# Softmax shifts of two causal attentions: made by GpSimd instead of VectorE, the second half's maximum seeded with the first's

## The chip, the cores and the metric

The kernel runs on one core of one Trainium2 chip. The metric is the device time of one execution in microseconds (us); lower is better. Engines are called as in the profile: PE is TensorE (PEld its weight loads), DVE is VectorE, ACT is ScalarE, POOL is GpSimd, SP is SyncE, which issues the DMAs.

## What is computed

A chain of six blocks over x of shape (2, 1024, 512), in fp32. Two of them are causal self-attentions, and only these are touched:

```python
x = x + 0.5 * ffn(layernorm(x))          # low-rank corrected product, scaled per column
x = x + attention_0(layernorm(x))        # 32 query heads of 16, 8 key heads, rotary: "rot"
x = x + 0.5 * ffn(layernorm(x))
x = x + 0.5 * moe(layernorm(x))          # 8 experts of rank 16, top 2
x = x + attention_1(layernorm(x))        # 8 heads of 32: "std"
x = x + 0.5 * moe(layernorm(x))
# inside an attention, per head:
scores = q @ k.T * scale; scores = where(causal, scores, -big)
out = softmax(scores) @ v
```

## The kernel before

The two batches run one after the other, with the six blocks in sequence. All five engines run programs of their own, in an order written out by hand, and meet through semaphores. An attention treats its heads in units: rot has 8 units of 4 heads, std 4 units of 2 heads. For each unit there are two streams of work.

**The stream of scores.** Twelve steps per unit: 4 for the first half of the queries (c=0), 8 for the second (c=1), each step one block of 128 keys. In a step TensorE makes transposed scores (`score`, L742 in rot, L736 in std), ScalarE takes their exponential (L1149), GpSimd sets to zero what is above the diagonal, in steps on the diagonal only (`affine_select`, L1301), and two steps later (rot) or three (std) TensorE multiplies by the values (`value`, L758). In this layout a query is a column, so the row maximum can't be subtracted by an operand of the exponential. It enters as two further rows of the queries' operand, a high and a low part ("the shifts"), which are multiplied by ones on the keys' side.

**The stream of maxima.** For those shifts the maximum of each query row has to be known before its scores are made, about one unit ahead. TensorE makes the scores once more in the other layout (`ring_item`, L660) into three PSUM banks that are used in turn ("the ring"), and VectorE reduces each bank to a column of `maxes`: by `tensor_reduce` (L949) where no mask is needed, or by a fused add of the causal mask and maximum (L945, a main instruction and a read of the accumulator) where the bank holds the diagonal. A query tile t has one bank set for the first 512 keys (kp=0) and, for t of 4 to 7, a second one for the rest (kp=1, always masked). In a rot unit that is 16 `tensor_reduce` of 512 columns and 32 masked ones, 16 of them with kp=1; in a std unit 8, 16 and 8.

After the last bank of t=3 (c=0) and of t=7 (c=1) of a unit, `shift_parts` makes the shifts of those four query tiles from `maxes`, on VectorE: for c=1 first the maximum of the two halves (L981, 128x16 in rot), then the negative rounded to the short format (L985), then what the rounding left (L987). An item of the ring ("shift") has TensorE transpose them (L665), VectorE copy them out (L958) and SP write them as rows into the queries' operand (L490). The item stands `SHIFT_DELAY` banks behind the bank that it depends on. Items "norm" divide finished heads by their sums (L670 on TensorE, L965 and L970 on VectorE).

`plan_ring` writes the order of the ring's items against the steps: `ring_first` before the first step (12 banks and `SHIFT_DELAY` and a slack of 12 in rot, 6 and the same in std), then three slots per step. TensorE takes the items in that order between its `score` and `value`, and waits for VectorE to have read the item three before it (`ring_free`).

## Time and profile before

| what | value |
|---|---|
| median of 3 runs | 1426.17 us (1425.89 to 1436.26) |
| the profiled execution | 1425.2 us, of which the span of its instructions is 1423.5 us |
| PE busy | 1298.5 us, 91% |
| DVE busy | 963.8 us, 68% |
| ACT busy | 630.8 us, 44% |
| POOL busy | 485.5 us, 34% |
| rot attention | about 137 to 402 us and 837 to 1100 us |
| std attention | about 555 to 650 us and 1250 to 1348 us |
| granted TensorE clock, mean | 0.933 of full speed |

The busy time is an average over very different stages. The rot attentions, more than a third of the time, have two engines busy over 90% of the time side by side; the layers between them have TensorE alone. A granted clock of 1.00 is 2.4 GHz and of 0.50 is 1.2 GHz.

### The profile page before, as it was taken

What the parts mean: (1) busy time and instruction counts of PE and PEld (TensorE: products, weight loads), DVE (VectorE), ACT (ScalarE), POOL (GpSimd) and SP (SyncE); (2) the same over time, 40 slices, a digit from 0 to 9 for tenths busy, and PEclk for the clock granted to TensorE, in tenths of its full rate; (3) what the DMA queues carried; (4) which work ended last, traced back from release to release, by engine and by line L of the source; (5) the groups of instructions that cost most, each with busy time, mean ns of one, the idle gap of its engine ahead of it and who ended that gap; (6) DMA issues with size and microseconds to landing.
All of it is one profiled execution on the core that took longest, in us unless ns stands there. A gap on an engine that the chain in (4) does not pass through costs nothing.

```text
span 1423.5 us, 21475 instructions
## 1 busy us (share of the span) xinstructions
PE 1298.5 (91%) x7328; PEld 799.1 (56%) x7328; DVE 963.8 (68%) x2846; ACT 630.8 (44%) x929; POOL 485.5 (34%) x734
## 2 busy tenths in 40 slices
PE   4997999999899898998879889999988999999898
PEld 1875544444277686445658754444434877854366
DVE  5765898899257845644758467999871787376276
ACT  1245366666622245443212544766665222634421
POOL 1574032221255442116426621311223653311261
PEclk8999599999999998999989975999999999989999
DMA  9200000110011000000130000010100100000001
GB/s 299 88 1 30 2 2 2 32 32 3 1 35 37 1 1 30 2 1 5 55 144 1 24 8 2 3 32 2 32 3 1 56 15 1 31 2 2 1 16 45
DMA packets 19932, 38.50 MB, mean 27 GB/s; under 512 B 4416, under 2 KB 6208, under 8 KB 19712
## 3 DMA queue, kind: packets, MB, share of 16 engines
q1 hardware_dynamic: 19824, 37.12, 7.8%
q8 instruction: 60, 0.98, 0.3%
q14 instruction: 48, 0.39, 0.1%
HBM read 31.21 MB, written 11.01 MB: 30 GB/s over the span
## 4 chain that ended last, share of the span: by engine, by line
PE 68%; DVE 17%; POOL 5%; issue 5%; ACT 3%; DMA 2%; SPq 0%; DVEq 0%; ACTq 0%; POOLq 0%
PE bank L758 15%; PE bank L660 12%; PE bank L587 7%; PE bank L589 7%; PE bank L588 7%; DVE maxes L949 5%; PE bank L742 4%; PE bank L640 4%; PE bank L736 3%; DVE unused L945 3%; PE bank L567 2%; PE bank L622 2%; PE bank L670 2%; POOL probs L1221 2%; DVE x L847 1%
## 5 line engine op out<-in xcount | busy, mean ns | idle before, releaser
L1149 ACT ACTIVATE probs<-bank 128x1024 f32<-128x1024 f32 (+3 forms) x416 | 368.0, 911 | 301.5 <-PE bank L742 192.5
L660 PE MATMUL bank<-ops 48*128 48x512 f32 (+3 forms) x960 | 323.5, 441 | 13.3 <-DVE maxes L949 4.1
L945 DVE CUSTOM_DVE_ANT_0 unused<-bank,causal 128x128 bf16<-128x128 f32 (+3 forms) x640 | 279.4, 486 | 73.0 <-PE bank L660 69.8
L1301 POOL TENSOR_SCALAR_AFFINE_SELECT probs<-probs 128x256 f32<-128x256 f32 (+1 forms) x256 | 118.8, 464 | 587.6 <-ACT probs L1149 587.3
L660 PEld LDWEIGHTS bank<-ops 48*128 48x128 f32 (+1 forms) x960 | 164.2, 208 | 198.1 <-DVE maxes L945 79.6
L758 PE MATMUL bank<-probs,v_mem 128*17 128x512 f32 (+6 forms) x1920 | 256.1, 524 | 6.1 <-ACT heads_raw L1138 5.6
L949 DVE TENSOR_REDUCE maxes<-bank 128x1 f32<-128x512 f32 x320 | 207.3, 684 | 40.3 <-PE bank L660 38.8
L1051 ACT CAST xT<-bank 128x512 fp32r<-128x512 f32 (+1 forms) x128 | 71.2, 560 | 271.7 <-PE bank L567 271.7
L742 PE MATMUL bank<-ops 50*128 50x512 f32 (+2 forms) x640 | 178.5, 454 | 4.9 <-ACT probs L1149 4.8
L822 DVE TENSOR_TENSOR xT<-bank,xT 128x512 fp32r<-128x512 f32 (+1 forms) x128 | 83.5, 655 | 125.0 <-ACT xT L1051 124.9
L587 PE MATMUL bank<-w_odd_hi,xT 128*128 128x512 f32 (+1 forms) x384 | 155.4, 405 | 1.9 <-DVE xT L822 1.9
L589 PE MATMUL bank<-w_odd_hi,xT 128*128 128x512 f32 (+1 forms) x384 | 138.0, 359 | 0.0
L588 PE MATMUL bank<-w_odd_lo,xT 128*128 128x512 f32 (+1 forms) x384 | 137.7, 359 | 0.0
L742 PEld LDWEIGHTS bank<-ops 50*128 50x128 f32 x640 | 88.0, 200 | 58.2 <-ACT probs L1149 29.7
L1106 ACT CAST ops<-bank 128x512 fp32r<-128x512 f32 x144 | 81.7, 587 | 65.9 <-PE bank L640 65.7
L587 PE MATMUL bank<-ops,xT 128*128 128x512 f32 x224 | 100.3, 448 | 4.0 <-DVE x L847 1.6
L640 PE MATMUL bank<-identf,features 128*128 128x128 f32 x512 | 78.5, 290 | 19.5 <-POOL heads_raw L1258 13.9
L1191 POOL TENSOR_SCALAR var_eps<-mv 128x1 f32<-128x1 f32 x96 | 38.9, 405 | 159.1 <-DVE mv L805 158.9
L589 PE MATMUL bank<-ops,xT 128*128 128x512 f32 x224 | 90.1, 402 | 0.0
L588 PE MATMUL bank<-ops,xT 128*128 128x512 f32 x224 | 89.8, 401 | 0.0
L758 PEld LDWEIGHTS bank<-probs,v_mem 128*17 128x17 f32 (+1 forms) x1920 | 41.0, 99 | 78.0 <-issue 52.6
L640 PEld LDWEIGHTS bank<-identf,features 128*128 128x128 f32 x512 | 62.4, 147 | 37.7 <-POOL heads_raw L1258 17.3
(109 smaller groups left out, 1896.1 us busy)
## 6 DMA issues: line engine op xcount, KB each, us to landing
w_odd_lo<-staging_wqkv SPq DMA_DIRECT2D x4, 1536.0 KB, 6.7
x<-x_dram SPq DMA_DIRECT2D x16, 256.0 KB, 5.9
out_dram<-x SPq DMA_DIRECT2D x16, 256.0 KB, 2.0
staging_wqkv<-wqkv_dram SPq DMA_DIRECT2D x2, 1536.0 KB, 14.0
ops<-staging_dora SPq DMA_DIRECT2D x3, 1024.0 KB, 5.5
ops<-shiftT SPq DMA_DIRECT2D x160, 4.0 KB
w_odd_lo<-staging_wo SPq DMA_DIRECT2D x2, 1024.0 KB, 5.2
ops<-staging_base SPq DMA_DIRECT2D x2, 1024.0 KB, 5.5
```

What stands on the lines that cost most here:

```text
L587: mm(dst, x_hi[:, k, :], hi[:, k, :], start=(k == 0), stop=False)
L588: mm(dst, x_hi[:, k, :], lo[:, k, :], start=False, stop=False)
L589: last = mm(dst, x_lo[:, k, :], hi[:, k, :], start=False, stop=(k == kc - 1 and not lora))
L640: last = nc.tensor.transpose(dst[:, k * P:(k + 1) * P], src, identf[:])
L660: last = mm(dst[:, h * w:(h + 1) * w], queries(a, u)[rows, t // 4, hi, t % 4 * P:(t % 4 + 1) * P], keys(a, u, hi)[rows, HALF * kp:HALF * k ...
L742: last = mm(dst, keys(a, u, 0)[rows, block], queries(a, u)[rows, c, heads_of[0]:heads_of[-1] + 1, columns], start=True, stop=True)
L758: last = mm(heads[a.head_rows * h:a.head_rows * h + a.dim + 1, q0 - HALF * c:HALF], v[:, j, a.kv_head(u, r, i), :], probs[:, e % 6, n, fir ...
L822: V.tensor_tensor(xT[:, n % 2, 1, 0:kc, :], turn[n % 2][:, 0:kc * P].rearrange("p (k c) -> p k c", k=kc), xT[:, n % 2, 0, 0:kc, :].bitcast ...
L945: V.tensor_tensor_reduce(unused[:, masked % 3, 0:w], part, causal[:, HALF - w:], 1.0, NEG, ALU.add, ALU.max, dst).then_inc(s["max_done"].s ...
L949: V.tensor_reduce(dst, part, AX.X, ALU.max).then_inc(s["max_done"].sem, 1)
L1149: A.activation(probs[:, e % 6, :, 0:cols], scores[:, 2 * (e % 2):2 * (e % 2) + 2, 0:cols], ACT.Exp, scale=a.scale).then_inc(s["exp"].sem, 1)
L1301: G.affine_select(out=p, in_=p, compare_op=ALU.is_ge, fill=0.0, base=0, pattern=pattern, channel_multiplier=-1).then_inc(s["masked"].sem, 1)
```

## The change

`shift_parts` moves from VectorE's program to GpSimd's. Its work there is three instructions for each half: minus the maximum into a new buffer `minus_max`, a cast of it to the short format (the high part), and the difference of the two (the low part). GpSimd makes them in its `attention` loop, after the masks of the step in which the half's last bank was put into the ring (`maxima_by_step`); those of banks in `ring_first` it makes before its first mask. It waits for that bank's maxima (`max_done`), and from the second unit on also for the transposition of the unit before (`ring_full`).

The combining maximum (L981) is gone. Instead the masked maximum of kp=1 starts from the one that kp=0 gave for the same head and tile: the immediate start value `NEG` becomes a column of `maxes`, which VectorE reads per partition, behind a further wait on its own `max_done`.

`SHIFT_DELAY` goes from 3 to 5, so a shift item stands two banks later in the ring, and `ring_first` is two banks longer.

```diff
-SHIFT_DELAY = 3
+SHIFT_DELAY = 5
...
                 if n + 1 in self.max_banks_of:
+                    self.maxima_by_step[step[0]].append((u, self.max_banks_of.index(n + 1)))
                     due_m.append([(u, self.max_banks_of.index(n + 1)), SHIFT_DELAY])
...
-                                V.tensor_tensor_reduce(unused[:, masked % 3, 0:w], part, causal[:, HALF - w:], 1.0, NEG,
+                                above = NEG
+                                if kp == 1:
+
+                                    m0 = a.max_bank_of(t, 0, head)
+                                    dve.wait_ge(s["max_done"].sem, s["max_done"].at(b, u * a.unit_max_ops + a.max_ops_to[m0]))
+                                    above = maxes[:, u % 2, 0, a.heads.index(head), t:t + 1]
+                                V.tensor_tensor_reduce(unused[:, masked % 3, 0:w], part, causal[:, HALF - w:], 1.0, above,
                                                        ALU.add, ALU.max, dst).then_inc(s["max_done"].sem, 1)
...
-                        if n + 1 in a.max_banks_of:
-                            shift_parts(b, st, u, a.max_banks_of.index(n + 1))
...
-                if c == 1:
-                    V.tensor_tensor(mx, mx, maxes[:, u % 2, 1, 0:nh, 4:8], ALU.max).then_inc(s["shift_step"].sem, 1)
-                    dve.wait_ge(s["shift_step"].sem, s["shift_step"].at(b, 3 * u + 2))
...
-                V.tensor_scalar(hi, mx, -1.0, None, ALU.mult).then_inc(s["shift_step"].sem, 1)
-                dve.wait_ge(s["shift_step"].sem, s["shift_step"].at(b, 3 * u + 1 + 2 * c))
-                V.scalar_tensor_tensor(lo, mx, -1.0, hi.bitcast(F32), ALU.mult, ALU.subtract).then_inc(s["shift"].sem, 1)
...
+            def shift_parts(b, st, u, c):
+
+                a, s = ATT[st], qs[st]
+                nh, m = a.unit_heads, a.unit_heads * 4
+                ch = 2 * u + c
+                mx = maxes[:, u % 2, c, 0:nh, 4 * c:4 * c + 4]
+                pool.wait_ge(s["max_done"].sem, s["max_done"].at(b, u * a.unit_max_ops + a.max_ops_to[a.max_banks_of[c] - 1]))
+                if ch >= 2:
+
+                    pool.wait_ge(s["ring_full"].sem, s["ring_full"].at(b, a.ring.index(("shift", u - 1, c)) + 1))
...
+                G.tensor_scalar(minus, mx, -1.0, None, ALU.mult).then_inc(s["shift_step"].sem, 1)
+                pool.wait_ge(s["shift_step"].sem, s["shift_step"].at(b, 2 * ch + 1))
+                G.tensor_copy(hi, minus).then_inc(s["shift_step"].sem, 1)
+                pool.wait_ge(s["shift_step"].sem, s["shift_step"].at(b, 2 * ch + 2))
+                G.tensor_tensor(lo, minus, hi.bitcast(F32), ALU.subtract).then_inc(s["shift"].sem, 1)
...
+                    for unit, c in a.maxima_by_step[g + 1]:
+                        shift_parts(b, st, unit, c)
```

How this moves instructions, at three places. In these rows `unused,maxes<-bank,causal` is the masked maximum (its second row reads the accumulator), and L958, L960, L964 and so on are lines of the changed file where it is of the change.

VectorE, the end of a rot unit's maxima (t=7, kp=1) and the start of the next, before:

```order
L945 ISA unused,maxes<-bank,causal 128x512 [waits rot_max_done,rot_ring_full]
L945 ISA maxes 128x1
L945 ISA unused,maxes<-bank,causal 128x512 [waits rot_max_done,rot_ring_full]
L945 ISA maxes 128x1
L981 TENSOR_TENSOR maxes<-maxes 128x4x4 [waits rot_max_done]
L985 TENSOR_SCALAR shifts<-maxes 128x16 [waits rot_shift_step]
L987 SCALAR_TENSOR_TENSOR shifts<-maxes,shifts 128x16 [waits rot_shift_step]
L945 ISA unused,maxes<-bank,causal 128x128 [waits rot_max_done,rot_ring_full]
```

and of the change:

```order
L960 ISA unused,maxes<-bank,causal,maxes 128x512 [waits rot_max_done,rot_ring_full]
L960 ISA maxes 128x1
L960 ISA unused,maxes<-bank,causal,maxes 128x512 [waits rot_max_done,rot_ring_full]
L960 ISA maxes 128x1
L960 ISA unused,maxes<-bank,causal,maxes 128x512 [waits rot_max_done,rot_ring_full]
L960 ISA maxes 128x1
L960 ISA unused,maxes<-bank,causal 128x128 [waits rot_max_done,rot_ring_full]
L960 ISA maxes 128x1
```

The three small instructions are gone, and the masked maxima of kp=1 have `maxes` among what they read.

TensorE, step 4 of a rot unit (the shift of the next unit's c=0), before, where L660 is a bank of the ring, L665 the transposition of the shifts, L742 a score, L758 a value:

```order
L742 MATMUL bank<-ops 128x512 [waits rot_exp_done,rot_shift_rows1]
L742 MATMUL bank<-ops 128x512
L660 MATMUL bank<-ops 128x512 [waits rot_max_done] x2
L665 MATMUL bank<-identf,shifts 32x128 [waits rot_shift_ready,rot_heads_ready]
L742 MATMUL bank<-ops 128x512 [waits rot_exp_done]
L742 MATMUL bank<-ops 128x512
L660 MATMUL bank<-ops 128x512 [waits rot_max_done]
L758 MATMUL bank<-probs,v_mem 17x256 [waits rot_exp_done,rot_masked]
```

and of the change, with L669, L674, L751 and L767 in their places:

```order
L751 MATMUL bank<-ops 128x512 [waits rot_exp_done,rot_shift_rows1]
L751 MATMUL bank<-ops 128x512
L669 MATMUL bank<-ops 128x512 [waits rot_max_done] x2
L751 MATMUL bank<-ops 128x512 [waits rot_exp_done]
L751 MATMUL bank<-ops 128x512
L669 MATMUL bank<-ops 128x512 [waits rot_heads_ready]
L767 MATMUL bank<-probs,v_mem 17x256 [waits rot_exp_done,rot_masked]
L767 MATMUL bank<-probs,v_mem 17x256 x3
L669 MATMUL bank<-ops 128x128 [waits rot_max_done]
L669 MATMUL bank<-ops 128x128
L674 MATMUL bank<-identf,shifts 32x128 [waits rot_shift_ready,rot_max_done]
```

The transposition stands two banks later, behind a score, a value and their waits.

GpSimd, the first masks of the first rot attention, before:

```order
L1301 AFFINE_SELECT probs<-probs 128x2x128 [waits rot_exp_done] x4
L1301 AFFINE_SELECT probs<-probs 128x4x128 [waits rot_exp_done]
L1301 AFFINE_SELECT probs<-probs 128x2x256 [waits rot_exp_done]
L1301 AFFINE_SELECT probs<-probs 128x2x128 [waits rot_exp_done] x4
L1301 AFFINE_SELECT probs<-probs 128x4x128 [waits rot_exp_done]
```

and of the change:

```order
L1294 TENSOR_SCALAR minus_max<-maxes 128x16 [waits rot_max_done]
L1296 CAST shifts<-minus_max 128x16 [waits rot_shift_step]
L1298 TENSOR_TENSOR shifts<-minus_max,shifts 128x16 [waits rot_shift_step]
L1318 AFFINE_SELECT probs<-probs 128x2x128 [waits rot_exp_done] x4
L1294 TENSOR_SCALAR minus_max<-maxes 128x16 [waits rot_max_done]
L1296 CAST shifts<-minus_max 128x16 [waits rot_shift_step]
L1298 TENSOR_TENSOR shifts<-minus_max,shifts 128x16 [waits rot_shift_step]
L1318 AFFINE_SELECT probs<-probs 128x4x128 [waits rot_exp_done]
L1294 TENSOR_SCALAR minus_max<-maxes 128x16 [waits rot_ring_full,rot_max_done]
L1296 CAST shifts<-minus_max 128x16 [waits rot_shift_step]
L1298 TENSOR_TENSOR shifts<-minus_max,shifts 128x16 [waits rot_shift_step]
L1318 AFFINE_SELECT probs<-probs 128x2x256 [waits rot_exp_done]
```

Three instructions stand ahead of the first mask; further threes stand behind the masks of steps 1, 2 and 10, and from the second unit on behind those of steps 2 and 10.

## Rows read from the trace of the kernel before

**Rows 1.** The page: span, busy time and share of each engine.

```profile
span 1423.5 us, 21475 instructions
...
PE 1298.5 (91%) x7328; PEld 799.1 (56%) x7328; DVE 963.8 (68%) x2846; ACT 630.8 (44%) x929; POOL 485.5 (34%) x734
```

**Rows 2.** Windows, four units: us; busy PE, PEld, DVE, ACT, POOL; clock; DMA.

```profile
307.65:335.89 28.24, 27.48 (x197) 11.70 (x197) 26.28 (x91) 19.00 (x22) 5.79 (x13) 1.00 0.13 41
...
1003.35:1032.76 29.41, 28.86 (x197) 12.07 (x197) 26.29 (x92) 18.99 (x22) 5.80 (x13) 0.94 0.13 38
...
248.78:279.39 30.61, 30.05 (x197) 12.41 (x197) 26.48 (x92) 18.97 (x22) 5.80 (x13) 0.89 0.12 37
...
607.03:628.93 21.90, 20.71 (x104) 10.31 (x102) 14.88 (x52) 10.66 (x14) 3.26 (x9) 1.00 0.00 1
```

**Rows 3.** Windows, stretches inside a rot unit and at rot's start (columns likewise).

```profile
318.01:327.97 9.96, 9.49 (x66) 4.56 (x69) 9.76 (x30) 7.57 (x9) 0.00 (x0) 1.00 0.04 14
...
329.31:339.99 10.68, 10.49 (x81) 4.17 (x77) 9.98 (x38) 7.12 (x8) 3.53 (x8) 1.00 0.01 2
...
137.30:161.90 24.60, 22.68 (x62) 12.91 (x65) 24.28 (x86) 6.13 (x7) 2.27 (x5) 0.54 0.01 2
```

**Rows 4.** Chain that ended last, 335 to 350 us: start, us, what.

```profile
336.24 0.81 PE bank L758 x8
...
339.03 0.56 PE bank L758 x8
```

**Rows 5.** Timeline, all engines, 335.6 to 338.4 us: start, us, engine, line.

```profile
335.88 0.64 POOL L1301 TENSOR_SCALAR_AFFINE_SELECT probs<-probs 128x512 f32<-128x512 f32 x1 [1.84 <-ACT probs L1149]
...
335.89 0.65 DVE L981 TENSOR_TENSOR maxes<-maxes 128x16 f32<-128x16 f32 x1
...
336.98 0.64 POOL L1301 TENSOR_SCALAR_AFFINE_SELECT probs<-probs 128x512 f32<-128x512 f32 x1 [0.46 <-ACT probs L1149]
...
337.64 0.28 PE L665 MATMUL bank<-identf,shifts 128*32 128x128 f32 x1
```

**Rows 6.** Timeline of VectorE, 317.5 to 350 us.

```profile
318.01 1.29 DVE L949 TENSOR_REDUCE maxes<-bank 128x1 f32<-128x512 f32 x2 [0.67 <-PE bank L660]
...
339.99 0.56 DVE L945 CUSTOM_DVE_ANT_0 unused<-bank,causal 128x384 bf16<-128x384 f32 x1
...
343.99 0.17 DVE L985 TENSOR_SCALAR shifts<-maxes 128x16 fp32r<-128x16 f32 x1
...
346.26 1.29 DVE L949 TENSOR_REDUCE maxes<-bank 128x1 f32<-128x512 f32 x2 [0.66 <-PE bank L660]
```

**Rows 7.** Chain at the end of rot's last maxima, 360 to 367 us.

```profile
364.16 0.66 DVE maxes L981
...
365.05 0.19 DVE shifts L987
...
365.37 0.27 PE bank L665
```

**Rows 8.** Timeline of GpSimd's mask there.

```profile
364.14 0.64 POOL L1301 TENSOR_SCALAR_AFFINE_SELECT probs<-probs 128x512 f32<-128x512 f32 x1 [1.85 <-ACT probs L1149]
```

**Rows 9.** Single lines on VectorE: duration ns min/median/max, first and last start, forms.

```profile
L985 DVE TENSOR_SCALAR shifts<-maxes x48: 171/175/672, 138.6 to 1324.7; 128x16 fp32r<-128x16 f32 x32, 128x8 fp32r<-128x8 f32 x16
...
L981 DVE TENSOR_TENSOR maxes<-maxes x24: 166/651/656, 155.7 to 1324.5; 128x16 f32<-128x16 f32 x16, 128x8 f32<-128x8 f32 x8
...
L869 DVE TENSOR_SCALAR route<-route x32: 153/154/155, 451.0 to 1416.7; 128x1 f32<-128x1 f32 x32
...
L872 DVE TENSOR_SCALAR gate<-expert_no,top_atf,route x32: 290/291/293, 451.6 to 1417.2; 128x8 f32<-128x8 f32 x32
```

**Rows 10.** Single lines on GpSimd, likewise.

```profile
L1191 POOL TENSOR_SCALAR var_eps<-mv x96: 211/437/808, 20.9 to 1395.0; 128x1 f32<-128x1 f32 x96
...
L1258 POOL TENSOR_TENSOR heads_raw<-probs,heads_raw x16: 442/454/1035, 86.1 to 829.0; 128x128 fp32r<-128x128 f32 x16
```

**Rows 11.** Waits of TensorE: total us, times, longest.

```profile
PE bank L665 <- DVE shifts L987: 7.7, 4, 2.4
```

24 lines of the change are left out of this document (13 added, 11 removed).

## The prediction

> **What bounds the kernel now.** The page comes first: a span of 1423.5 us with PE busy for 91% and DVE for 68% [rows 1]. The second number is a mean over unlike stages, so the next view is the windows of single units. A steady unit of rot takes 28.24 us at full clock, with DVE busy for 26.28 of them and PE for 27.48; a unit of std takes 21.90 us with DVE busy for 14.88 only [rows 2]. So an edit on DVE can count in rot, which has 14 such units of maxima (units 1 to 7 in both batches; unit 0 is made at rot's start), and hardly in std.
>
> Inside a rot unit I read VectorE's timeline for its idle gaps, since a busy engine with gaps is waiting. There are two kinds of stretch. From 318.01 to 327.97 us DVE is busy for 9.76 of 9.96 us; it is in front of this stretch that it waited 0.67 us for PE, so the stretch begins when PE lets it begin and ends when DVE is through: it is DVE's. It holds the maxima of t=4 and t=5 and the start of t=6 [rows 3, 6]. From 329.31 to 339.99 DVE is busy for 9.98 of 10.68 us and waits for PE in between and at the end, while PE is busy for 10.49: this one is PE's [rows 3, 6].
>
> The shift instructions of the old kernel lie in the second kind. L981, L985 and L987 run from 335.89 to about 336.97, and there the chain of work that ended last goes through PE's value matmuls (336.24 for 0.81 us) [rows 4, 5]. The half c=0 runs at 343.99, and behind it DVE stands idle for 0.66 us, until 346.26 [rows 6]. On the chain they are only at a rot attention's start and at the end of its last maxima [rows 7].
>
> **What is removed from VectorE.** Per rot unit five instructions. Each of the plain ones is 0.175 us; L981 is 0.166 us at best and 0.651 in the median [rows 9], where it runs beside a mask of GpSimd that starts within 0.01 us of it [rows 5]. From one to the next go some 0.035 us (from 364.16 to 365.24 the three take 1.08 [rows 7]). That makes 0.45 us for c=0 and 1.05 for c=1, so 1.5 us per unit, 21 us of DVE's time over the 14 units.
>
> The Trainium skill, "SBUF — State Buffer", section "Who interferes with whom", states that a VectorE instruction with two inputs in SBUF and a GpSimd instruction that reads SBUF lock each other out; the 651 against 166 ns agree. By it 0.49 us per unit, 6.8 of the 21, are such a lock, and GpSimd's mask gets its share back too; with DVE's own times alone the sum would have 14 us here.
>
> What is it worth? In a steady unit the work hiding it is PE's, in stretches where PE is busy without a break. DVE will idle 1.2 us instead of 0.1 at 339.99 and 1.1 instead of 0.66 at 346.26. The most that can come back is what PE's weight loads gain by finding their bank free earlier; I take 0.1 us per unit, 1.4 us in all, and 0.7 per unit (10 us) as the bound. At a rot attention's start, 137.3 to 161.9, DVE is busy for 24.28 of 24.60 us [rows 3], and there five instructions at 0.21 us each are saved in full: 1.0 us, twice.
>
> **What is added to VectorE.** The masked maxima of kp=1 now read their start value per partition. No masked maximum of the trace does so. The nearest rows are two `tensor_scalar` lines: with immediates 154 ns on one element (L869) and 175 ns on up to 16 (L985), with two columns as scalars 291 ns on eight elements (L872) [rows 9]. Two such operands cost 116 ns over L985, one 58 if they add up. Lower bound 0, if the fetch lies in the overlap with the accumulator read of the instruction before; upper bound 137 ns, if one operand costs what the pair costs over L869. I take 58, half of the nearest pair.
>
> The Trainium skill, "ScalarE: Activation LUTs", section "What ACT_TABLE_LOAD costs", gives about 93 ns for each such operand on ScalarE; no run here shows that. By it, as an estimate, the next sum would be 10.4 us instead of 6.5.
>
> Sixteen instructions per rot unit get the operand. The eight of t=4 and t=5 lie in DVE's stretch and are paid in full: 8 x 0.058 x 14 = 6.5 us. The eight of t=6 and t=7 lie in PE's stretch, where DVE has gaps, and are free as long as they stay under what the removal gave; at 116 ns they are 0.93 us per unit against 1.05. At a rot attention's start all sixteen are on the path: 0.93 us, twice, which cancels the 1.0 saved there. Std has eight per unit, beside an engine that is idle a third of the time: nothing. The added wait on `max_done` names an instruction at least three before in rot, two in std, each of 0.2 to 0.6 us: long done, nothing.
>
> **What is added to GpSimd.** Three instructions per half, 144 in all. GpSimd is busy for 5.79 of 28.24 us in a rot unit [rows 2], so only the place counts. A `tensor_scalar` on one column is 0.21 us at least and 0.44 in the median, a `tensor_tensor` on 128 columns 0.45 in the median [rows 10]. Three with their waits are between 0.9 and 1.4 us; I take 1.2. Two things stand behind them. The transposition (L665) ran at 337.64 [rows 5]. GpSimd's mask of that step ends at 336.52, the shifts are ready at 337.7, and the order has the transposition two banks later, past 338.3: in time, by over 0.6 us. The next mask, which ran at 336.98, is pushed to 337.7 to 338.4; the value that reads it ran at 339.03 [rows 4, 5]: in time by 0.6. SP's queue, which writes the rows, is asked later by two banks, half a unit or so before the scores need them: nothing.
>
> At the end of an attention's last maxima nothing covers the chain. The shift item follows its bank at once, as nothing is left to put between, and PE waits for it already: four waits, 7.7 us [rows 11]. In rot DVE had it ready at 365.24 [rows 7]; GpSimd starts its mask at 364.14, is through at 364.78 [rows 8] and with the shifts at 366.0: 0.8 us later. In std L981 is not slowed, but most of the mask is over by then; I take 0.7. Together 2 x 0.8 + 2 x 0.7 = 3.0 us.
>
> **Two banks more before the first step.** They move 1.2 us of DVE's work ahead of the first score. In rot DVE is the bound there anyway and does them a step later otherwise. In std it may cost that once per batch; I leave it at nothing.
>
> **The sum.** +6.5 for the operand, 0.0 at rot's starts, +3.0 at the ends, -1.4 for weight loads: +8.1 us. On the profiled execution's 1425.2 that is 1433.3. The median of the runs lies 1.0 above that execution, so the forecast is 1434.
>
> **The granted clock.** In [rows 2] one unit takes 30.61 us at 0.89 and another 29.41 at 0.94, against 28.24 at 1.00, with the same 26.3 to 26.5 us of DVE's work. Of twelve periods between steady units three were of the first kind and two of the second, about 9.5 us in all. The fall to 1.2 GHz comes behind DVE's stretch, in which PE waits much. A stretch half a microsecond longer may bring more of it, a shorter one less. I forecast as many as before, and carry 7 us either way.
>
> **Rivals.**
>
> *The operand is hidden* (chance 0.25, no change). Then the 6.5 goes: +1.6, 1428. For it speaks that the masked maxima overlap with each other's accumulator read; against it that L872 shows a cost at all.
>
> *The removal pays and the clock stays up* (0.12, faster). The operand is hidden, PE takes up to 0.7 us per unit (-10), the 9.5 us of lost clock come back, and the ends cost 3.0: 1426.2 - 16.5, about 1410. Against it: DVE idles where the removal lies [rows 6].
>
> *The operand costs double and spreads* (0.22, slower). At 116 ns the eight in DVE's stretch are 13 us; at 137, with those of t=6 and t=7 half exposed, 15.3 + 7.7 = 23. With the ends, and the clock's 7 in the worse half, 1441 to 1459. It becomes slower by 1% from about 100 ns on. The mechanism is VectorE as the bound of rot's units through t=4 and t=5.
>
> *GpSimd is late* (0.08, slower). If the three take over 1.8 us, the mask behind them misses its value at 339.03, and PE stands in each unit. At the maxima of [rows 10] (0.81, 0.81 and 1.04) they are 2.7 us: 0.9 x 14 + 1.5 x 4 = 19 us on top of the sum, 1453.
>
> The forecast itself has 0.33. That the change doesn't do what it says is out: the order of instructions shows both parts.
>
> **How the numbers follow.** 1% is 14 us, about what a measurement of this kernel can tell from no change. Faster by more: 0.12. Within 1%, 1412 to 1440: the forecast and the hidden operand, 0.58. Slower: 0.22 + 0.08 = 0.30. The range leaves out most of the fast rival and the far end of the slow ones: 1418 to 1450.
>
> **What would show it.** In the changed profile: the masked maxima of kp=1 by some 60 ns longer than those of kp=0 at 128, 256, 384 and 512 columns; DVE's stretch over t=4 and t=5 longer by half a microsecond; rot units at 28.7 us at full clock; DVE's idle time in the second half of a unit up by a microsecond; the waits of L665's successor for GpSimd four times, near 2.8 us each at most in rot, and none elsewhere. It is wrong if kp=1 costs nothing extra, if a steady unit at full clock is under 28 us, or if values wait for masks in every unit.

## The result and the profile after

Six runs of the changed kernel have a median of 1450.47 us (1440.37 to 1466.83), six of the kernel before beside them 1433.15 us (1425.89 to 1436.26). The ratio is 1.0119, with a 95% interval from 1.0079 to 1.0158: slower by 1.2%. Runs more than 1.5% above the fastest of their kernel are left out of every ratio, and of the means further below: one of the six here, two of six in e3, three of twelve in e1 and e5, six of twelve in e9, and at most one elsewhere.

The forecast was 1434 us with a range of 1418 to 1450. The sum said 8 us more than before, and the two medians differ by 17: the sign is right, the size half of what it should be, and the result lies just beyond the 1% within which most of the chance was put. In the absolute time, 7 of the 16 us between 1434 and 1450 come from the base: the forecast stood on three runs with a median of 1426.17, and the six beside the changed kernel have 1433.15.

The profiled execution took 1441.55 us. Its page, span and busy time, to be read beside [rows 1]:

```profile
span 1439.8 us, 21619 instructions
...
PE 1302.8 (90%) x7328; PEld 801.5 (56%) x7328; DVE 953.2 (66%) x2726; ACT 628.6 (44%) x929; POOL 515.2 (36%) x878
```

VectorE has 10.6 us less to do than before and GpSimd 29.7 more, and the kernel is slower. Windows of single units show a part of it. The columns are those of [rows 2]: a rot unit at full clock, the rot unit before it, and a std unit:

```profile
287.50:315.93 28.43, 27.18 (x195) 11.75 (x196) 25.91 (x86) 18.77 (x23) 7.01 (x19) 1.00 0.01 3
256.21:287.50 31.29, 30.26 (x195) 12.90 (x196) 26.29 (x86) 18.88 (x23) 7.02 (x19) 0.84 0.10 34
596.50:619.21 22.71, 21.61 (x108) 10.41 (x107) 14.38 (x46) 10.64 (x15) 4.46 (x14) 1.00 0.01 1
```

Two readings follow. At full clock a rot unit takes 28.43 us against 28.24, so little is lost there. But of the ten periods from unit 2 to unit 7 of the two batches six take 31.3 us at a mean granted clock of 0.84. And a std unit takes 22.71 us against 21.90, at full clock both times, with less on VectorE.

The five periods from unit 2 to unit 7 in one window, first of the changed kernel (first and second batch):

```profile
193.47:344.32 150.85, 145.20 (x971) 62.71 (x972) 130.46 (x430) 94.48 (x112) 37.14 (x94) 0.90 0.05 16
896.63:1047.46 150.83, 145.17 (x971) 62.75 (x972) 130.46 (x431) 94.48 (x112) 37.16 (x94) 0.90 0.05 16
```

and of the kernel before:

```profile
197.37:344.29 146.92, 143.24 (x960) 60.55 (x957) 131.91 (x456) 94.82 (x110) 29.00 (x61) 0.93 0.06 17
...
897.66:1041.16 143.50, 139.98 (x970) 59.05 (x969) 131.46 (x457) 94.64 (x111) 30.24 (x62) 0.98 0.06 17
```

Ten full-clock units are 284.3 us in the changed kernel and 282.4 before; what was measured is 301.7 and 290.4. So 1.9 of the 11.3 us lost here lie at full clock and 9.4 in the clock.

The period from unit 1 to unit 2, just ahead of these, went the other way. First the changed kernel, then the one before, first and second batch each:

```profile
165.41:193.47 28.06, 26.83 (x191) 11.31 (x184) 25.31 (x86) 20.24 (x26) 10.03 (x20) 0.98 0.01 2
868.59:896.63 28.04, 26.81 (x191) 11.29 (x184) 25.30 (x86) 20.23 (x26) 10.03 (x20) 0.99 0.01 2
...
165.41:197.37 31.96, 31.35 (x200) 13.74 (x197) 27.52 (x91) 21.04 (x26) 9.97 (x15) 0.82 0.01 2
864.86:897.66 32.80, 32.49 (x190) 14.58 (x186) 26.49 (x91) 21.04 (x26) 8.76 (x14) 0.72 0.01 2
```

Here the changed kernel is 8.7 us shorter, so over all twelve periods it is behind by 2.6 us of the 16.3 by which the two profiled spans differ. One execution of each kernel therefore doesn't show where the time goes; the experiments below, which have many runs, have to.

The groups of VectorE by shape, where those with `maxes` among the inputs are kp=1:

```profile
L960 DVE CUSTOM_DVE_ANT_0 unused<-bank,causal,maxes 128x512 bf16<-128x512 f32 x80 | 57.0, 746 | 6.2 <-PE bank L669 5.3
...
L960 DVE CUSTOM_DVE_ANT_0 unused<-bank,causal 128x512 bf16<-128x512 f32 x80 | 51.4, 686 | 19.6 <-PE bank L669 19.6
...
L960 DVE CUSTOM_DVE_ANT_0 unused<-bank,causal,maxes 128x128 bf16<-128x128 f32 x80 | 24.4, 341 | 0.3
...
L960 DVE CUSTOM_DVE_ANT_0 unused<-bank,causal 128x128 bf16<-128x128 f32 x80 | 18.8, 287 | 19.8 <-PE bank L669 19.8
```

The operand costs 60 ns at 512 columns and 54 at 128. GpSimd's three instructions stand in the timeline behind the mask that ends at 336.66:

```profile
336.63 0.25 POOL L1294 TENSOR_SCALAR minus_max<-maxes 128x16 f32<-128x16 f32 x1
...
336.95 0.20 POOL L1296 CAST shifts<-minus_max 128x16 fp32r<-128x16 f32 x1
...
337.23 0.22 POOL L1298 TENSOR_TENSOR shifts<-minus_max,shifts 128x16 fp32r<-128x16 f32 x1
337.41 0.65 POOL L1318 TENSOR_SCALAR_AFFINE_SELECT probs<-probs 128x512 f32<-128x512 f32 x1
```

They take 0.82 us from first start to last end, and the next mask runs at 337.41, 1.39 us behind the start of the mask before it; in the kernel before that distance was 1.10 us (335.88 to 336.98, [rows 5]). The waits of TensorE for shifts, beside [rows 11], and for the rows in the std attention (the second is of its weight loads):

```profile
PE bank L674 <- POOL shifts L1298: 11.4, 6, 2.7
...
PE bank L767 <- POOL probs L1318: 0.4, 2, 0.2
```

```profile
PEld bank L745 <- DMA ops<-shiftT: 10.2, 6, 1.9
```

In the kernel before the second wait stood once, for 1.7 us. The timeline of a std unit shows how it comes about:

```profile
591.88 0.28 PE L674 MATMUL bank<-identf,shifts 128*16 128x128 f32 x1
...
592.70 0.27 DVE L971 COPY shiftT<-bank 16x128 f32<-16x128 f32 x1
...
593.00 1.31 SPq L499 DMA_DIRECT2D ops<-shiftT  x2
...
595.48 0.74 PE L745 MATMUL bank<-ops 98*128 98x512 f32 x2 [0.69 <-DMA ops<-shiftT]
...
596.26 1.02 ACT L1147 ACTIVATE probs<-bank 128x1024 f32<-128x1024 f32 x1 [2.38 <-PE bank L745]
```

From the transposition to the first score that reads the rows go 3.6 us. Two banks later in the ring is a step later in std, and the score waits; ScalarE, which waits for that score, stands idle for 2.38 us.

### The profile page after: what moved, and what is told of

Same layout as the page of the kernel before. It is cut to its first block, busy times and chain, and to the rows that moved or that the text cites. A ratio compares the mean times of both kernels' runs of the same rounds, so it can differ in the third digit from the quotient of the medians.

```text
span 1439.8 us, 21619 instructions
## 1 busy us (share of the span) xinstructions
PE 1302.8 (90%) x7328; PEld 801.5 (56%) x7328; DVE 953.2 (66%) x2726; ACT 628.6 (44%) x929; POOL 515.2 (36%) x878
## 4 chain that ended last, share of the span: by engine, by line
PE 68%; DVE 15%; POOL 5%; issue 5%; ACT 4%; DMA 2%; SPq 0%; DVEq 0%; ACTq 0%; POOLq 0%
PE bank L767 14%; PE bank L669 13%; PE bank L596 7%; PE bank L598 7%; PE bank L597 7%; PE bank L751 5%; DVE maxes L964 4%; PE bank L649 4%; PE bank L745 3%; PE bank L576 2%; PE bank L679 2%; PE bank L631 2%; ACT probs L1147 2%; DVE unused L960 2%; DVE x L856 2%
## 5 line engine op out<-in xcount | busy, mean ns | idle before, releaser
L669 PE MATMUL bank<-ops 48*128 48x512 f32 (+3 forms) x960 | 326.5, 441 | 15.1 <-DVE maxes L964 8.4
L669 PEld LDWEIGHTS bank<-ops 48*128 48x128 f32 (+1 forms) x960 | 169.5, 211 | 197.3 <-DVE maxes L960 81.3
L767 PE MATMUL bank<-probs,v_mem 128*17 128x512 f32 (+6 forms) x1920 | 263.4, 536 | 6.2 <-ACT heads_raw L1136 5.2
L964 DVE TENSOR_REDUCE maxes<-bank 128x1 f32<-128x512 f32 x320 | 204.9, 681 | 49.8 <-PE bank L669 49.0
L751 PE MATMUL bank<-ops 50*128 50x512 f32 (+2 forms) x640 | 183.2, 458 | 5.0 <-ACT probs L1147 4.8
L960 DVE CUSTOM_DVE_ANT_0 unused<-bank,causal 128x128 bf16<-128x128 f32 (+3 forms) x320 | 138.2, 487 | 60.8 <-PE bank L669 60.7
L960 DVE CUSTOM_DVE_ANT_0 unused<-bank,causal,maxes 128x128 bf16<-128x128 f32 (+3 forms) x320 | 161.7, 543 | 24.8 <-PE bank L669 23.6
L751 PEld LDWEIGHTS bank<-ops 50*128 50x128 f32 x640 | 89.8, 203 | 57.4 <-ACT probs L1147 30.0
L767 PEld LDWEIGHTS bank<-probs,v_mem 128*17 128x17 f32 (+1 forms) x1920 | 41.7, 100 | 81.2 <-issue 49.9
```

The source lines that it names most:

```text
L669: last = mm(dst[:, h * w:(h + 1) * w], queries(a, u)[rows, t // 4, hi, t % 4 * P:(t % 4 + 1) * P], keys(a, u, hi)[rows, HALF * kp:HALF * k ...
L751: last = mm(dst, keys(a, u, 0)[rows, block], queries(a, u)[rows, c, heads_of[0]:heads_of[-1] + 1, columns], start=True, stop=True)
L767: last = mm(heads[a.head_rows * h:a.head_rows * h + a.dim + 1, q0 - HALF * c:HALF], v[:, j, a.kv_head(u, r, i), :], probs[:, e % 6, n, fir ...
L960: V.tensor_tensor_reduce(unused[:, masked % 3, 0:w], part, causal[:, HALF - w:], 1.0, above, ALU.add, ALU.max, dst).then_inc(s["max_done"] ...
L964: V.tensor_reduce(dst, part, AX.X, ALU.max).then_inc(s["max_done"].sem, 1)
```

## The experiments

Every kernel was timed in five rounds beside the kernel before. "Rot unit" is the distance between two first `tensor_reduce` of neighbouring units, with the mean granted clock of that distance.

**First set: the change taken apart.** e1 has only the delay: `SHIFT_DELAY = 5` in the kernel before.

> The kernel before with SHIFT_DELAY 5 and nothing else: shifts stay on VectorE, no seed. Theory A (the late item): in std the item of the shifts moves from step 12 to step 13 of a unit, its rows land after the scores of step 16 are due, and TensorE waits for the DMA three times per std attention, 0.4 to 0.7 us idle each with ScalarE idle for 2.4; in rot the transposition stands where the ring is full and TensorE idles 0.46 us per unit. Then this kernel alone is 6 to 12 us slower than before. Theory B (the per-partition start value is what costs, as in the prediction): within 2 us of before. Theory C (GpSimd is late): within 2 us of before too, since GpSimd does nothing new.

Measured: ratio 1.0021 [0.9994, 1.0048]. Windows of a rot and of a std unit:

```profile
285.23:313.27 28.04, 26.94 (x195) 11.95 (x196) 26.27 (x92) 18.78 (x23) 5.83 (x12) 1.00 0.01 3
592.66:615.33 22.67, 21.57 (x108) 10.41 (x107) 14.85 (x51) 10.66 (x15) 3.27 (x8) 1.00 0.01 2
```

The delay does two things that nearly cancel: a rot unit gets 0.2 us shorter, a std unit 0.8 longer. The late rows are the delay's, not GpSimd's. The first theory had the waits right, but its total of 6 to 12 us did not come, since it had no gain in rot.

e2 has only the start value: kp=1 seeded, L981 gone, the two other instructions still on VectorE, delay 3.

```diff
-                if c == 1:
-                    V.tensor_tensor(mx, mx, maxes[:, u % 2, 1, 0:nh, 4:8], ALU.max)...
+                                if kp == 1:
+                                    above = maxes[:, u % 2, 0, a.heads.index(head), t:t + 1]
```

> The kernel before with the seeded maximum alone: kp=1 starts from the maximum of kp=0, L981 is gone, the other two shift instructions stay on VectorE, SHIFT_DELAY 3. Theory A: no transfer becomes late in std, and the time is within 4 us of before. Theory B: 60 ns for each of 16 instructions per rot unit against 0.69 us for L981 gone; the eight in VectorE's stretch cost 0.5 us per unit, 14 units, so 4 to 10 us slower, with more of the low clock in units 3 to 5 of rot.

Measured: 1.0171 [1.0146, 1.0195], the largest cost of any part. A rot unit, five of them (unit 2 to 7) and a std unit:

```profile
293.32:322.99 29.67, 29.09 (x195) 12.04 (x195) 27.05 (x92) 19.18 (x23) 5.83 (x12) 0.94 0.05 9
...
200.82:354.57 153.75, 151.00 (x970) 62.91 (x969) 136.09 (x452) 95.56 (x111) 30.39 (x62) 0.88 0.05 16
...
606.13:627.99 21.86, 21.45 (x108) 10.46 (x107) 15.04 (x51) 10.66 (x15) 3.27 (x8) 1.00 0.01 2
```

VectorE has 27.05 us of work against 26.28 in [rows 2], and no steady rot unit of the profiled execution is wholly at full clock. Std is untouched. The ratio stands for 24 us, where the expectation had 4 to 10.

e3 is the changed kernel with `SHIFT_DELAY = 3`, e4 the changed kernel with 5 in rot and 3 in std.

> The changed kernel with SHIFT_DELAY back at 3 in both attentions. Theory A: std is as before the change, the waits for the rows and the 0.46 us per rot unit are gone, so 6 to 12 us faster than the changed kernel (0 to 8 us over before). But the shifts of GpSimd are ready 0.8 us after the mask, so TensorE may wait for them at rot's item, up to 0.5 us per unit, which would eat up to 7 of it. Theory B: as slow as the changed kernel, 14 to 20 us over before.

> The changed kernel with SHIFT_DELAY 3 in std and 5 in rot. Theory A: only the std part is mended, and the waits of std's scores for the rows are gone: 6 to 9 us faster than the changed kernel, so 8 to 11 over before. Theory B: no difference from the changed kernel.

Measured: e3 1.0157 [1.0119, 1.0195], e4 1.0095 [1.0058, 1.0132]. The old delay did not make the changed kernel faster, against the first theory. A full-clock rot unit of e3:

```profile
967.37:996.05 28.68, 27.96 (x195) 11.84 (x196) 26.05 (x86) 19.18 (x23) 7.07 (x19) 1.00 0.07 26
```

At the old delay the changed kernel has the unit of 28.7 us that the prediction named; at the new one it is 28.43. In e4 the std units are back at 21.89 us; its ratio is 3 us under that of the change, within the intervals of both.

e5 is the changed kernel without the start value (the maximum of the halves is made on VectorE again, GpSimd waits for it), e6 the same with delay 3, which is the move to GpSimd alone.

> The changed kernel without the seed: the masked maxima of kp=1 start from the immediate again, VectorE combines the two halves in one instruction per unit (as L981 did), GpSimd makes the shifts from that, SHIFT_DELAY 5. Theory A (late item): std keeps its waits for the rows, so still 8 to 14 us over before. Theory B (operand): the 60 ns go, 7 to 10 us faster than the changed kernel, and the low clock in rot's units 3 to 5 returns to short stretches.

> The move to GpSimd alone: SHIFT_DELAY 3, no seed, VectorE keeps the one combining instruction. Both the operand and the late item are gone. If A and B are all there is, within 3 us of before plus the 3 us of the attentions' ends. If theory C (GpSimd is late for an item three banks behind) holds, TensorE waits for GpSimd at the transposition in each rot unit and it is 5 us or more over before.

Measured: e5 1.0046 [1.0008, 1.0083], e6 0.9967 [0.9939, 0.9995]. A rot unit of e6:

```profile
314.73:342.98 28.25, 27.48 (x195) 11.72 (x196) 25.73 (x88) 19.00 (x23) 7.11 (x19) 1.00 0.09 32
```

VectorE has 0.55 us less, and the unit is as long as before to 0.01 us. So at full clock the removal is worth nothing, and GpSimd is late nowhere in a steady unit. The interval of e6 lies just under 1 all the same. e5 is 10 us faster than the changed kernel by the ratios, as the second theory had it: this is what the start value costs there.

**Second set: the operand by itself.** e7 is the kernel before, with a constant column as the start value of all maxima of kp=1; e8 has it in all masked maxima.

```diff
+            V.memset(floor[:], NEG).then_inc(s_const.sem, 1)
...
+                                above = floor[:, :] if kp == 1 else NEG
-  ... causal[:, HALF - w:], 1.0, NEG,
+  ... causal[:, HALF - w:], 1.0, above,
```

> The kernel before, with the start value of the masked maxima of kp=1 read from a constant column of -1e30 in place of the immediate. Nothing else changes, so this is the operand by itself: 320 instructions, 60 ns longer each. Theory B: 6 to 14 us slower than before. Theory A: under 4 us. The two differ by whether VectorE's time in t=4 and t=5 sets a rot unit's time.

> As the one before, with the column read by all 640 masked maxima, so twice the operand cost: 1.9 us more of VectorE per rot unit. If VectorE is the bound throughout, the loss doubles against e7 or more (15 to 30 us over before). If only t=4 and t=5 count, the added operands of t=0 to 3 lie where VectorE has gaps, and it is at most 4 us slower than e7.

Measured: e7 1.0175 [1.013, 1.0219], e8 1.0334 [1.03, 1.0368]. A rot unit of e7 at full clock, and unit 2 to unit 7:

```profile
292.73:321.43 28.70, 27.97 (x195) 11.87 (x195) 27.03 (x92) 19.19 (x23) 5.80 (x12) 1.00 0.04 8
...
199.45:352.32 152.87, 149.84 (x970) 62.83 (x968) 136.01 (x456) 95.55 (x111) 30.23 (x62) 0.90 0.05 16
```

and unit 2 to unit 7 of e8:

```profile
204.27:366.29 162.02, 157.58 (x961) 65.95 (x960) 140.96 (x457) 95.82 (x110) 29.00 (x61) 0.84 0.05 15
```

The operand alone, with nothing that depends on another instruction, costs as much as the seed. At full clock it adds 0.46 us to a unit (8 x 0.058 was 0.46), which is 6.4 us for 14 units, and the ratio says 25 us; the expectation had 6 to 14. I had expected that e8 adds at most 4 us to e7, since its other operands lie in TensorE's stretch; its one unit at full clock is indeed no longer (28.72 us), but the kernel takes 23 us more. This is where "hidden at full clock" and "free" part.

e11 and e12 split e7 by place: the column only at t=4,5 (`kp == 1 and t in (4, 5)`), or only at t=6,7.

> The kernel before with a constant column as start value only in the masked maxima of the second key half of t=4,5, which lie in the stretch where VectorE is busy without a pause. By place (an operand costs where VectorE has no idle time and nothing elsewhere): all of the cost of e7_column_kp1, a full-clock unit of 28.70 us and a ratio of 1.010 to 1.019. By the clock (any added VectorE time lowers it): about half of it, 1.006 to 1.010.

> The same only for t=6,7, which lie where VectorE still has idle time. By place, as the prediction had it: nothing, a full-clock unit of 28.25 us and a ratio of 0.998 to 1.002. By the clock: a full-clock unit of 28.25 to 28.30, but more units at a low clock, ratio 1.005 to 1.010.

Measured: e11 1.0136 [1.0094, 1.0178], e12 1.0048 [1.0024, 1.0073]. Neither theory alone: the place matters by a factor near three, but t=6,7 is not free. Together they make 1.0184, near the 1.0175 of e7. Two neighbouring units of e12:

```profile
251.87:280.21 28.34, 27.55 (x195) 11.65 (x195) 26.65 (x92) 18.97 (x23) 5.80 (x12) 1.00 0.07 25
280.21:310.88 30.67, 30.08 (x195) 12.40 (x195) 26.83 (x92) 18.96 (x23) 5.80 (x12) 0.89 0.04 6
```

**Third set: what brings the clock down.** e13 adds time of VectorE without any operand: behind the last masked maximum of kp=1 of t=4 and t=5 of a rot unit

```diff
+                                    V.tensor_scalar(spare[:, t - 4:t - 3], minus_half[:, :], -1.0, None, ALU.mult)
```

> The kernel before with two small VectorE instructions more in each rot unit, behind the last masked maximum of kp=1 of t=4 and of t=5; each multiplies one column of a constant into a spare tile that nobody reads (no operand, no wait). By the nearest row they are 0.15 us each, with the step between instructions some 0.38 us per unit, near the 0.45 that the operand added. If VectorE's time in that stretch is what counts: a full-clock unit of 28.55 to 28.65 us, units of 30 to 32 us at a low clock in most places, ratio 1.008 to 1.018. If it is something of the operand: the full-clock unit is longer by the same, but no more low-clock units than before, ratio 1.002 to 1.006.

Measured: 1.0064 [1.0038, 1.0091]. A unit at full clock and its neighbour:

```profile
283.67:312.00 28.33, 27.61 (x195) 11.70 (x195) 26.37 (x95) 19.03 (x23) 5.83 (x12) 1.00 0.04 7
312.00:342.63 30.63, 30.08 (x196) 12.43 (x196) 26.61 (x95) 19.06 (x23) 5.83 (x12) 0.89 0.09 33
```

The two instructions last 149 ns each but start together with an accumulator read, so they add only 0.09 us to VectorE and as much to the unit: 0.09 x 14 is 1.3 us, and the ratio stands for 9. My expectation had both the size of the addition and that of its full-clock cost too high, and fell between its two cases. Its mean clock over twelve runs is 0.922, against 0.931 for 24 runs of the kernel before beside it on the same chip. So no operand is needed for a lower mean clock: a little more of VectorE's time there is enough. But where in the execution the clock is lost, e13 doesn't show: in its profiled execution units 2 to 7 take 289.7 us, against 290.4 before, with four of ten periods at a lowered clock against five.

e14 to e16 make three matmuls of the ring twice in each rot unit (the last one of each bank of kp=1 of t=4 and t=5), in the kernel before, in the changed one, and in e10.

```diff
+                        if kp == 1 and t in (4, 5) and len(a.heads) == 4 and h + 1 == len(heads_in):
+                            last = mm(dst[:, h * w:(h + 1) * w], ...the same operands..., start=True, stop=True)
```

> The kernel before with three matmuls of the ring made twice in each rot unit (the last one of each bank of kp=1 of t=4 and of t=5: 128, 256 and 256 columns), so that TensorE works some 0.3 us more just where it waits for VectorE; the result is the same. If TensorE's waits are what brings the clock down: fewer low-clock units than before, a mean clock above 0.933 and a ratio of 0.990 to 0.998. If not: a full-clock unit longer by 0 to 0.3 us and as many low ones, ratio 1.000 to 1.005.

> The changed kernel with the same three matmuls made twice. If TensorE's waits are the link from the operand to the clock: most of the units at 31.3 us go back to 28.4 to 28.7, ratio to the kernel before 1.000 to 1.008. If not: the ratio of the change, 1.010 to 1.018.

> The kernel before with the rot attention's delay at 5 (e10) and the same three matmuls made twice. Nearly all rot units of e10 were at full clock, so little is left to win: ratio 0.990 to 0.995 if the fill is free and keeps the rest up too, 0.995 to 1.001 if it costs TensorE its time.

Measured: e14 1.0009 [0.9977, 1.0041], e15 1.0129 [1.0075, 1.0183], e16 0.9917 [0.9885, 0.9948] against 0.9929 of e10. The unit of e14 at full clock:

```profile
285.18:313.54 28.36, 27.69 (x199) 12.03 (x199) 26.29 (x93) 19.07 (x23) 5.80 (x12) 1.00 0.04 9
```

It is 0.1 us longer, and the changed kernel with the fill still has five of ten such periods at 31.3 to 31.5 us. The idea that TensorE's small waits in that stretch are the link found no support in the times. It is not refuted either: three matmuls may be too few, and e16, measured on another chip than e10, has the highest mean clock of all kernels.

**Fourth set: the parts that pay.** e9 is e5 with the delay split (5 in rot, 3 in std): shifts on GpSimd, no start value. e10 is the kernel before with the same split and nothing else.

```diff
-SHIFT_DELAY = 3
+SHIFT_DELAY = {"rot": 5, "std": 3}
```

> The shifts on GpSimd without the start value (the masked maxima stand as before the change, the two maxima are combined on VectorE), and the delay of the shift item split: 5 steps in the rot attention, 3 in the std one. If the two costs found so far are all there is (the operand through the clock, and the late rows of the std attention) and the rot attention's gain at the longer delay is real, the rot units take 28.05 us at full clock, the std ones 21.89, and the ratio to the kernel before is 0.990 to 0.997. If the gain of the rot units is given back at the attentions' ends, it is 0.998 to 1.003.

> The kernel before with the rot attention's delay alone set to 5, shifts on VectorE. If the gain is the delay's and not GpSimd's: rot units 28.06 us, std units 21.89, ratio 0.992 to 0.999. If the move to GpSimd carries it: 0.999 to 1.003.

Measured: e9 0.9901 [0.9855, 0.9946], e10 0.9929 [0.9902, 0.9957]. e9 scatters widely (1407.66 to 1442.44 over twelve runs), and the median of all twelve, 1430.47, is that of the kernel before beside it (1431.81), so a gain of e9 is not shown. I would take e10: 1420.21 us, with 1415.94 to 1428.95 over twelve. Unit 2 to unit 7 of rot, and a std unit, of e10:

```profile
193.32:332.97 139.65, 134.09 (x967) 59.30 (x960) 131.42 (x457) 93.56 (x111) 30.39 (x62) 1.00 0.06 18
...
590.94:612.79 21.85, 21.44 (x108) 10.45 (x107) 14.86 (x51) 10.65 (x15) 3.27 (x8) 1.00 0.01 2
```

All five periods are at full clock. The kernel before needed 146.92 and 143.50 us for them.

**The clock in numbers.** Each run lists its mean granted clock, so time and clock can be set against each other. Over 91 runs of the kernel before (1418.5 to 1444.7 us at 0.938 to 0.913) a straight line fits: 9.8 us for each 0.01 of mean clock, with a scatter of 1.4 us around it and a correlation of -0.96. Its own runs thus differ by hardly anything but the clock. With that line the difference of each kernel's mean to the mean of before (1429.6 us at 0.9290) splits into what its clock explains and a rest:

| kernel | runs | mean clock | difference, us | by the clock | rest |
|---|---|---|---|---|---|
| the change | 5 | 0.918 | +17.9 | +10.4 | +7.5 |
| e1 delay | 9 | 0.931 | +0.2 | -1.6 | +1.8 |
| e2 start value | 5 | 0.913 | +22.5 | +16.0 | +6.5 |
| e3 change, delay 3 | 4 | 0.917 | +19.7 | +12.2 | +7.5 |
| e4 change, std 3 | 5 | 0.920 | +11.0 | +8.8 | +2.2 |
| e5 move, delay 5 | 9 | 0.928 | +3.7 | +0.6 | +3.1 |
| e6 move | 11 | 0.938 | -5.7 | -8.2 | +2.6 |
| e7 column, kp=1 | 6 | 0.915 | +22.7 | +13.4 | +9.4 |
| e8 column, all | 6 | 0.900 | +47.4 | +28.3 | +19.0 |
| e11 column, t=4,5 | 6 | 0.908 | +24.0 | +20.4 | +3.6 |
| e12 column, t=6,7 | 12 | 0.923 | +10.1 | +6.0 | +4.1 |
| e13 spare work | 12 | 0.922 | +8.2 | +6.6 | +1.5 |
| e9 move, rot delay 5 | 6 | 0.937 | -10.0 | -8.1 | -1.9 |
| e10 rot delay 5 | 12 | 0.935 | -7.9 | -5.7 | -2.3 |
| e14 fill | 11 | 0.930 | +0.8 | -1.2 | +2.0 |
| e15 change, fill | 5 | 0.923 | +18.2 | +6.1 | +12.1 |
| e16 rot delay 5, fill | 8 | 0.941 | -12.3 | -11.2 | -1.1 |

The split is rough: it lends the slope of one kernel to others, pools runs of several chips (so the differences are not the ratios above times 1430), and the rests of the parts add up to those of the whole only within some 4 us. But its order is plain. The rest of e2 is 6.5 us, that of e6 2.6. Whatever adds to VectorE's work in the rot attention lowers the mean clock (e2, e7, e8, e11, e12, e13). The opposite does not hold as a rule: e6, which takes some away, has a higher one, but e5, which takes as much away at the longer delay, has not; and over all twelve runs of each the mean clock is 0.925 for e1, 0.925 for e5 and 0.927 for e9. Only for e10 do all twelve runs show that the longer delay in rot raises it.

**Where the low clock lies.** For each profiled execution: the ten periods from unit 2 to unit 7 of both batches, how many of them had a mean clock under 0.97, the two periods from unit 1 to unit 2, and what is left of the difference of the spans to that of before.

| kernel | span | ten periods, us | low | two periods, us | elsewhere |
|---|---|---|---|---|---|
| before | 1423.5 | 290.4 | 5 | 64.8 | 0 |
| e6 move | 1423.6 | 288.5 | 4 | 61.4 | +5.4 |
| e13 spare work | 1437.3 | 289.7 | 4 | 65.7 | +13.6 |
| e14 fill | 1425.2 | 286.9 | 3 | 59.5 | +10.4 |
| e12 column, t=6,7 | 1429.9 | 293.2 | 5 | 57.8 | +10.5 |
| e11 column, t=4,5 | 1451.2 | 308.1 | 10 | 63.7 | +11.1 |
| e7 column, kp=1 | 1450.1 | 304.1 | 6 | 64.5 | +13.1 |
| e2 start value | 1456.4 | 307.6 | 10 | 63.9 | +16.6 |
| e8 column, all | 1484.2 | 322.9 | 9 | 67.1 | +25.9 |
| e3 change, delay 3 | 1449.4 | 301.5 | 7 | 63.2 | +16.5 |
| the change | 1439.8 | 301.7 | 6 | 56.1 | +13.7 |
| e4 change, std 3 | 1442.3 | 298.9 | 5 | 56.5 | +18.7 |
| e15 change, fill | 1467.1 | 299.1 | 5 | 59.5 | +40.2 |
| e1 delay | 1426.2 | 279.4 | 0 | 64.4 | +14.1 |
| e5 move, delay 5 | 1423.0 | 280.5 | 0 | 61.4 | +12.8 |
| e10 rot delay 5 | 1416.6 | 279.3 | 0 | 58.2 | +10.8 |
| e16 rot delay 5, fill | 1417.1 | 281.3 | 1 | 58.5 | +9.1 |
| e9 move, rot delay 5 | 1438.2 | 301.2 | 7 | 60.3 | +8.5 |

The kernel before was quick elsewhere in its profiled execution, so every other one has some us more there, much of it in layers that no edit touches. In the ten periods the kernels with an operand at t=4 and t=5 (e11, e7, e2, e8, e3, the change, e4, e15) take 299 to 323 us, and all others but one 279 to 293. That one is e9: without any operand it has seven low periods, where e5, with the same program in rot, has none. So at either delay the operand makes low periods more likely, and single executions of one program differ as much as two kernels do. For e12 and e13 the loss in the ratios is not found in these periods.

## Why the prediction was right or wrong

**"+6.5 for the operand": right as it was worked out, at full clock.** The price was taken as 58 ns and is 51 to 60. Eight of them in DVE's stretch were to lengthen a unit by 0.46 us; e7 shows 28.24 to 28.70, which is 6.4 us for 14 units; the rests of e2 and e7, 6.5 and 9.4 us, lie there or somewhat above. The sentence behind it, from the Trainium skill's page "ScalarE: Activation LUTs", section "What ACT_TABLE_LOAD costs", put such an operand at about 93 ns on ScalarE; on VectorE no width here shows more than 62.

**The granted clock: here it failed.** The step reads: "The fall to 1.2 GHz comes behind DVE's stretch ... A stretch half a microsecond longer may bring more of it, a shorter one less. I forecast as many as before, and carry 7 us either way." The text named the direction and then set it to zero. Over the runs the clock stands for about 10 of the 18 us, and for 16 of 22 where only the start value is changed. In the profiled execution of the change 9.4 of the 11.3 us lost between unit 2 and unit 7 are of units at a low clock (the periods from unit 1 to 2 gave 8.7 back there). The operand's rival had its price doubled to reach such times; in fact the forecast's 58 ns was right, and what the operand does to TensorE's clock was not counted.

Two readings of that step were off as well. It counted 9.5 us of lost clock, but the two periods from unit 1 to unit 2, at 31.96 and 32.80 us, were 8 us over full-clock units by themselves. And the falls do not come behind VectorE's stretch, which goes from about 2 to 12 us after a unit's first `tensor_reduce`, but inside it, in the kernel before at 8 us, with TensorE busy for 7.98 of 8.22 us ahead of one:

```profile
257.18:265.40 8.22, 7.98 (x61) 3.86 (x64) 7.38 (x25) 6.00 (x8) 0.64 (x1) 1.00 0.24 90
265.40:272.20 6.80, 6.80 (x29) 2.20 (x21) 4.88 (x14) 2.59 (x3) 0.00 (x0) 0.50 0.01 1
```

**The eight operands of t=6 and t=7 "are free as long as they stay under what the removal gave": wrong.** e12 costs 1.0048 [1.0024, 1.0073] with them alone. Its unit at full clock is 0.1 us longer, and of the 10.1 us in the table the clock stands for 6.0. The changed kernel also had the removal, but e3, which has both, is no better than e2.

**"SP's queue, which writes the rows, is asked later by two banks, half a unit or so before the scores need them: nothing": wrong in std.** This was looked at in rot, where it holds. In std the transposition moves to 591.88, the score that reads the rows comes 3.6 us later and waits. A std unit is longer by 0.8 us, six or so of them make 5; e1 against e10, which differ in std's delay only, gives 1.8 + 2.3 = 4.1 us, and the change against e4 gives 7.5 - 2.2 = 5.3.

**What was not in the sum at all: the delay's gain in rot.** With the shift item two banks later a rot unit takes 28.04 us (e1, e10) for 28.24, and in both profiled executions all ten periods are at full clock. Over 14 units the 0.2 us are 2.8, over half of std's loss. That the full-clock sum of +8.1 still meets the rest of 7.5 is luck: errors of opposite sign. What in the later item shortens a rot unit was not looked into.

**"-1.4 for weight loads": nothing came.** In e6 the unit is 28.25 us. The gain of the move is in the clock instead, which the fast rival had as one of its three parts; the two others fell with e7 (the hidden operand) and with e6 itself (TensorE taking up the removal).

**"+3.0 attention ends": 1.3 there, and 2.4 at rot's starts.** The waits for shifts rose from 7.7 to 11.4 us, by 3.7, which looks like the forecast. But at the four ends they rose by 0.35 us in rot (2.36 to 2.71) and 0.31 in std (1.49 to 1.80), 1.3 us in all. The other two of the six waits are new, 1.20 us each, and lie at the starts of the two rot attentions, where the prediction had none. First one end before, then that end and a start of the change:

```profile
365.37 0.27 PE L665 MATMUL bank<-identf,shifts 128*32 128x128 f32 x1 [2.36 <-DVE shifts L987]
```

```profile
368.97 0.27 PE L674 MATMUL bank<-identf,shifts 128*32 128x128 f32 x1 [2.71 <-POOL shifts L1298]
...
158.80 0.37 PE L674 MATMUL bank<-identf,shifts 128*32 128x128 f32 x1 [1.20 <-POOL shifts L1298]
```

At the end of rot's maxima the mechanism is the one forecast: the shifts stand behind the same mask as in [rows 8], here at 367.39.

```profile
367.39 0.64 POOL probs L1318
368.02 0.23 POOL minus_max L1294
...
368.60 0.23 POOL shifts L1298
```

They are ready 0.8 us behind the end of that mask, where 1.2 was taken; this is the term that was too large. In steady rot units GpSimd was late nowhere: TensorE's value matmuls waited 0.4 us in all for masks over the execution.

**Rot's starts: "0.0".** About half a microsecond each. From the first `tensor_reduce` of unit 0 to that of unit 1 go 26.47 us before, 27.28 in e7, 27.15 in e6 and 27.01 in the change, twice in each and at a clock of 0.50 to 0.52. So the operand alone costs 0.8 (0.93 was forecast), but the move alone costs 0.7, where the removal was to save 1.0; the two waits of 1.20 us above lie in these units. The window that took 24.60 us at a clock of 0.54 in [rows 3] covers the same maxima in about as long,

```profile
137.30:162.20 24.90, 22.71 (x63) 13.11 (x66) 24.10 (x81) 6.01 (x7) 3.65 (x11) 0.53 0.01 2
```

and agrees that nothing large came or went; its end is set by hand.

What stays open is the link between VectorE and the clock. The Trainium skill, page "TensorE: Matmul & The Clock Gate", section "Part 1: The HAM clock gate", says that the chip gates TensorE's clock by how busy it has been. The busy times here do not bear it out: ahead of a fall TensorE is busy nearly throughout, as the changed kernel's windows show for the head of a unit (5.28 of 5.59 us) and for the 10.2 us at the lower level behind it,

```profile
256.21:261.80 5.59, 5.28 (x39) 2.60 (x39) 4.84 (x16) 3.18 (x4) 1.10 (x4) 1.00 0.51 178
261.80:272.00 10.20, 10.20 (x48) 4.26 (x47) 8.03 (x22) 5.54 (x7) 0.00 (x0) 0.50 0.01 2
```

and making it busier in the stretch of t=4 and t=5 (e14, e15) did not measurably keep the clock up. The profile's ends of matmuls are modelled, so a finer measure of its work might tell more. That more work of VectorE in a rot unit goes with a lower mean clock of the execution is shown (e7, e12, e13), and for the operand at t=4 and t=5 that the low clock lies in the rot units; by what quantity the clock is set is not.

## What to carry to other kernels

Where an engine feeds TensorE at its limit, a microsecond counted at full clock is not the price: e13 added 0.09 us to a unit and the kernel lost some seven times what that makes, with a lower mean clock. So before adding work to such an engine, look at how many periods of the loop already run at a lowered clock; if some do, price the addition with the clock too and not at nothing. Compare the mean clock over many runs, and do not judge by one profiled execution: e5 and e9 have the same program in rot, and none and seven low periods of ten.

Check the base as well: three runs of the kernel before had a median of 1426, six others 1433, and this 7 us is as much as the whole forecast change.

An operand read per partition in place of an immediate is 51 to 62 ns on a VectorE instruction here. It is a poor trade in an inner loop for one small instruction per unit outside it: 16 x 0.06 = 0.96 us against 0.65.

A delay that is one constant for two stages is two edits. Follow the moved item to its last reader in each stage by itself.

## What the runs showed of the hardware

- TensorE's clock falls in loops in which TensorE looks full: with 27.5 of 28.2 us busy, some periods of the same code run at 1.00 and others at 0.89, in the changed kernel at 0.84, and the execution's time follows its mean clock with 9.8 us for 0.01.
- Small instructions on VectorE behind an accumulator read start together with it: 149 ns long, they cost the engine some 45 ns (e13: 0.09 us for two).
- GpSimd's instructions on 128x16 take 0.25 (multiply), 0.20 (cast) and 0.22 us (subtract), 0.82 with their waits (the changed kernel); the prediction, from wider or one-column rows, had taken 1.2.
- The combining maximum on 128x16 stays at 656 ns in the median where GpSimd makes the shifts too (e6), against 166 at best: GpSimd's masks still run beside it. The group, single lines of e6 on VectorE:

```profile
L965 DVE TENSOR_TENSOR maxes<-maxes x24: 166/656/658, 157.2 to 1325.6; 128x16 f32<-128x16 f32 x16, 128x8 f32<-128x8 f32 x8
```
